# Expert rows of a mixture-of-experts layer in blocks of two 64-row halves instead of blocks of 128

## The chip, the core and the metric

The kernel runs on one core of one Trainium2 chip, as one program. The time is what the device takes for one execution, in microseconds (us). Five engines work side by side and meet at semaphores: TensorE (PE in the profile, with its weight loads as PEld), VectorE (DVE), ScalarE (ACT), GpSimd (POOL) and SyncE (SP, whose queue starts most transfers). Three runs of the kernel before gave 254.44, 252.72 and 254.32 us, median 254.32. All arithmetic is float32 but for a few small tables in bfloat16.

## What is computed

One decoder layer on 1024 tokens (8 tiles of 128) of width 256: latent attention, cross attention, and a feed-forward part, which is the part that changes. Cut to that part, the reference is:

```python
E, K, I, H = 16, 2, 176, 256                       # experts, chosen per token, hidden width, model width
x = hidden_states.reshape(-1, H)                   # 1024 tokens, layer-normed
scores = softmax(x @ gate_w.T)
topk_w, topk_idx = lax.top_k(scores, K)
combine = sum(one_hot(topk_idx, E) * topk_w[..., None], axis=1)
gu = einsum('th,ehj->etj', x, w_gate_up)           # 256 -> 352 per expert
h = silu(gu[..., :I]) * gu[..., I:]
y = einsum('eti,eih,te->th', h, w_down, combine)   # 176 -> 256 per expert
y = y + swiglu(x @ shared_gate_up) @ shared_down   # shared expert, for every token
```

Only the two experts of a token need be computed, so there are 2048 pairs of token and expert. For the inputs of the timed runs the sixteen experts get 69, 17, 81, 36, 112, 501, 135, 74, 592, 9, 104, 28, 62, 136, 18 and 74 of them (counted with the reference).

## The kernel before, in words

**Routing tables.** DVE, PE and POOL turn the router's choice into two lists of row numbers: for each row of a block the token to read (`idx[:, 0]`) and the place to write its result (`idx[:, 1]`). The pairs are sorted by expert, and every expert starts a new block of 128 rows, so 31 blocks are always enough (`BLOCKS`, L41). Here 25 hold rows; the last 6 are empty, but are computed all the same, since the program has no branch on the counts. The list of each block's expert (`bei`, L1549) is read by PE's sequencer into a register (`read_expert`, L917), and the register picks the weights in `gu_s` (up projection) and `dn_s` (down projection), which hold all sixteen experts.

**The expert loop.** A block of 128 rows passes through these steps: POOL gathers its rows from DRAM into one of four buffers (L487); PE transposes them with 2 products against the identity (`block_transpose`, L879) and DVE copies the result to `bxT` (`bT_out`, L1561); PE multiplies with the expert's up weights, 2 products over the two halves of the width (`expert_up`, L898); ACT takes the silu of one half (L1165), DVE multiplies it with the other (`h_mul`, L1567); PE transposes again (`hidden_transpose`, L889), ACT copies (`hT_out`, reported at L1000, the helper's line); PE multiplies with the down weights (`expert_down`, L910); ACT copies to `by` (`y_out`, L1000) and POOL scatters the rows to DRAM (L492). A float32 product appears as two records in the trace, a transpose as one. PE's order is written out (L974 to L987): in step i the hidden transpose of block i-2, the up projection of i, the row transpose of i+2, the down projection of i-3. Buffers alternate between two (PSUM banks, `bxT`, hidden) or four (`bx`, `by`).

**Around it.** The shared expert is worked in four pairs of token tiles with three column groups each (`shared_up`, L829, `shared_down`, L842). Two groups of the last pair stand behind the expert loop (L988, L989), and so do its 12 last products (L994). SP waits until every block with rows is back in DRAM (`written`, L385 to L387), then reads each token's two results (L389); DVE adds them with their weights (`weigh_pair`, L1574), adds the shared part (L1601), and SP and ACT write the output.

## Time and profile before

| | us |
|---|---|
| median of 3 runs | 254.32 |
| the profiled execution | 252.71 |
| its span, first to last instruction | 250.7 |
| PE busy in it, 1660 products | 237.4 |
| DVE busy | 148.5 |
| ACT busy | 129.3 |
| POOL busy | 92.5 |
| row gather of block 0 issued (L487) | at 157.61 |
| first up projection (L898) | at 164.43 |
| last output transfer issued (L1195) | at 248.32 |

Times in the rows further down count from the start of the span. A busy time of PE is the union of its records, and a record lasts beyond the moment at which the next product may start; the pace is therefore read from the starts. "idle before, releaser" in square brackets is how long the engine stood idle before a group and what ended it.

### The profile page before, as it was taken

To read this page: it belongs to the slowest core of one execution; us is meant where nothing else is said; L and a number is where in the kernel's file an instruction comes from. 1 tells how busy PE (TensorE), PEld (TensorE's weight loads), DVE (VectorE), ACT (ScalarE), POOL (GpSimd) and SP (SyncE) were. 2 spreads that over 40 slices of the span, in tenths; PEclk is the share of its full clock that TensorE was granted. 3 is DMA by queue.
4 is the path that set the end of the run, shared out by engine and by line. 5 is a ranking of instruction groups with operands and counts; after the bars stand their busy time and mean duration, and the time that the engine had idled before them with its cause. 6 is when DMAs were issued, how large, how long until landed. Compare 5 with 4: busy or idle time off the path is not lost.

```text
span 250.7 us, 5232 instructions
## 1 busy us (share of the span) xinstructions
PE 237.4 (95%) x1660; PEld 177.2 (71%) x1660; DVE 148.5 (59%) x452; ACT 129.3 (52%) x465; POOL 92.5 (37%) x110
## 2 busy tenths in 40 slices
PE   8969799999999999999999999799999999999995
PEld 6635475666766677898788787567777777777784
DVE  1568888887889856437896588653223232323184
ACT  2146988989889898540524216124343434343440
POOL 2111211112111100102662004655777777777460
PEclk9999999999999999999999999999999999999999
DMA  7999877100005400006013000222333333343495
GB/s 217 267 366 387 283 174 171 53 3 3 3 0 160 171 3 3 1 3 229 1 41 129 0 3 4 63 68 81 105 105 107 105 95 112 89 102 111 144 338 188
DMA packets 20388, 28.10 MB, mean 112 GB/s; under 512 B 2369, under 2 KB 17355, under 8 KB 20363
## 3 DMA queue, kind: packets, MB, share of 16 engines
q1 hardware_dynamic: 16683, 19.01, 24.5%
q0 software_dynamic: 2976, 8.13, 11.0%
q10 hardware_dynamic: 704, 0.64, 0.8%
q8 instruction: 14, 0.23, 0.4%
q14 instruction: 11, 0.09, 0.1%
HBM read 21.61 MB, written 6.16 MB: 111 GB/s over the span
## 4 chain that ended last, share of the span: by engine, by line
PE 71%; ACT 13%; DVE 8%; issue 4%; DMA 1%; POOL 1%; ACTq 0%; POOLq 0%; DVEq 0%
PE bank L898 15%; PE bank L910 11%; ACT pr_s L1010 10%; PE bank L829 8%; PE bank L531 5%; PE bank L573 4%; PE bank L560 3%; PE bank L879 3%; PE bank L889 3%; PE bank L658 2%; PE bank L536 2%; PE bank L623 2%; PE bank L649 1%; PE bank L668 1%; DMA qx_s<-ffn_in,prT 1%
## 5 line engine op out<-in xcount | busy, mean ns | idle before, releaser
L1010 ACT ACTIVATE pr_s<-bank,mx 128x128 f32<-128x128 f32 x128 | 45.2, 383 | 8.0 <-DVE mx L1236 8.0
L898 PE MATMUL bank<-gu_s,bxT 128*128 x124 | 41.7, 460 | 0.2 <-DVE bxT L1561 0.2
L1567 DVE TENSOR_TENSOR pr_s<-bank,pr_s 128x176 f32<-128x176 f32 x31 | 10.6, 341 | 51.6 <-ACT pr_s L1165 50.9
L492 POOL DMA_INDIRECT expert_out<-by,prT x31 | 31.0, 1000 | 14.8 <-ACT by L1000 7.5
L487 POOL DMA_INDIRECT qx_s<-ffn_in,prT x31 | 30.1, 972 | 14.6 <-issue 8.2
L1000 ACT ACTIVATE prT<-bank 128x512 f32<-128x512 f32 (+1 forms) x63 | 31.1, 497 | 2.9 <-PE bank L573 1.8
L910 PE MATMUL bank<-dn_s,prT 88*128 x124 | 31.7, 379 | 0.0
L1010 ACT ACTIVATION_READ_ACCUMULATOR pr_s<-bank,mx 128x1 f32 x128 | 28.6, 224 | 0.0
L898 PEld LDWEIGHTS bank<-gu_s,bxT 128*128 128x128 f32 x124 | 21.2, 190 | 7.2 <-issue 0.4
L1000 ACT ACTIVATE by<-bank 128x256 f32<-128x256 f32 x31 | 11.9, 383 | 23.5 <-PE bank L910 21.9
L1236 DVE TENSOR_REDUCE mx<-bank 128x4 f32<-128x512 f32 x32 | 20.5, 683 | 4.7 <-PE bank L560 4.7
L829 PE MATMUL bank<-ck_s,sgu_s 128*128 128x256 f32 (+1 forms) x96 | 22.0, 381 | 1.1 <-issue 1.1
L910 PEld LDWEIGHTS bank<-dn_s,prT 88*128 88x128 f32 x124 | 21.2, 190 | 2.2
L573 PE MATMUL bank<-tab,pr_s 128*128 128x128 f32 x128 | 19.5, 275 | 3.1 <-ACT pr_s L1010 2.7
L1165 ACT ACTIVATE pr_s<-bank 128x176 f32<-128x176 f32 x31 | 9.8, 317 | 24.3 <-PE bank L898 24.3
L573 PEld LDWEIGHTS bank<-tab,pr_s 128*128 128x128 f32 x128 | 15.0, 140 | 8.3 <-ACT pr_s L1010 4.0
L829 PEld LDWEIGHTS bank<-ck_s,sgu_s 128*128 128x128 f32 (+1 forms) x96 | 17.0, 181 | 4.6 <-issue 1.7
L414 POOL TENSOR_TENSOR rs<-ve,halfpow 128x2 f32<-128x2 f32 x8 | 5.6, 702 | 32.7 <-DVE ve L1276 32.7
L409 POOL TENSOR_TENSOR rs<-ve,halfpow 128x1 f32<-128x1 f32 x8 | 4.4, 554 | 33.3 <-DVE ve L1211 33.3
L1561 DVE COPY bxT<-bank 128x256 f32<-128x256 f32 x31 | 12.9, 415 | 3.7 <-PE bank L879 3.5
L1128 ACT ACTIVATE kbd<-bank 128x256 f32<-128x256 f32 (+1 forms) x12 | 4.6, 383 | 20.0 <-PE bank L829 20.0
L879 PEld LDWEIGHTS bank<-tab,qx_s 128*128 128x128 f32 x62 | 8.6, 140 | 8.1 <-issue 4.4
(194 smaller groups left out, 438.2 us busy)
## 6 DMA issues: line engine op xcount, KB each, us to landing
gu_s<-in_w_gu SPq DMA_DIRECT2D x8, 704.0 KB, 7.0
dn_s<-in_w_dn SPq DMA_DIRECT2D x4, 704.0 KB
gu_s<-in_ctx_in SPq DMA_DIRECT2D x2, 512.0 KB, 9.2
ffn_in<-x_s SPq DMA_DIRECT2D x4, 256.0 KB, 2.4
cv_s<-expert_out SPq DMA_DIRECT2D x4, 256.0 KB, 4.1
x_s<-expert_out SPq DMA_DIRECT2D x4, 256.0 KB, 5.7
out<-x_s SPq DMA_DIRECT2D x7, 128.0 KB, 3.6
gu_s<-in_x_t SPq DMA_DIRECT2D x1, 768.0 KB, 10.7
```

The lines of the kernel that those rows point to most:

```text
L487: pool.indirect_dma_start(bx[:, i % RB, :], None, ffn_in[:], bass.IndirectOffsetOnAxis(ap=idx[:, 0, i:i + 1], axis=0)).then_inc(dma_gather ...
L492: pool.indirect_dma_start(expert_out[:], bass.IndirectOffsetOnAxis(ap=idx[:, 1, k:k + 1], axis=0), by[:, k % RB, :], None).then_inc(dma_sc ...
L531: last = mm(bank[3][:, 0:NOPE + D], ckvT[:, b % 2, k, :], wkv_s[:, k, :], start=k == 0, stop=k == 1)
L573: last = tr(probs_bank(n)[:, h * T:(h + 1) * T], pr_s[:, n % 2, h, :], idf)
L829: last = mm(shared_bank(q, c)[0:r, 2 * j * T:2 * (j + 1) * T], sgu_s[:, k, j * SI + c * 128:j * SI + c * 128 + r], xfT[:, k, 2 * q:2 * q + ...
L879: last = tr(bank[6 + i % 2][:, k * T:(k + 1) * T], bx[:, slot, k * 128:(k + 1) * 128], idf)
L898: last = mm(bank[2 + i % 2][:, 0:2 * I], bxT[:, i % 2, k, :], gu_s[:, k, bass.ds(e, 1), :], start=k == 0, stop=k == KD - 1)
L910: last = mm(bank[4 + i % 2][:, 0:D], bhT[:, i % 2, k, :], dn_s[:, k, bass.ds(e, 1), :], start=k == 0, stop=k == 1)
L1000: copy = lambda o, i: nc.scalar.activation(o, i, ACT.Copy)
L1010: last = nc.scalar.activation(pr_s[:, n % 2, h, :], score_bank(n)[:, h * T:(h + 1) * T], ACT.Exp, bias=mx[:, n % 4, h:h + 1], accum_out=de ...
L1236: V.tensor_reduce(mx[:, n % 4, :], score_bank(n)[:].rearrange("p (h k) -> p h k", h=CH), op=ALU.max, axis=AX.X, negate=True).then_inc(dve_ ...
L1561: V.tensor_copy(bxT[:, i % 2, :, :].rearrange("p k t -> p (k t)"), bank[6 + i % 2][:, 0:D]).then_inc(dve_block_T, 1)
```

## The change

A block still has 128 rows, but they are two halves of 64, each with an expert of its own. The first 64 pairs of expert e lie in the upper half of block e, for e below 16, so that half's weights are known without a register. All further groups of 64 ("more" halves, at most 32) fill the lower halves of blocks 0 to 15, and both halves of blocks 16 to 23. There are 24 blocks (`BLOCKS`) and 48 halves (`HALVES`). With the counts above there are 26 "more" halves, so blocks 0 to 20 hold rows.

Each projection is now four products in place of two: 64 columns of weights-side data (`bxT[..., 0:HT]`, `bxT[..., HT:T]`) with output in partitions 0 to 63 or 64 to 127 of the same bank. The lower half takes its weights by register, the upper half by number. From block 16 on the upper half takes them from four staging buffers (`gu_x`, `dn_x`), which SP fills from DRAM with each expert's 352 KB and 176 KB; they lie over buffers of the first part of the layer (`early`). The weights lie in DRAM with the rows of a partition together.

PE, ACT and DVE go through the blocks in pairs. The second group of the last shared pair moves from behind the loop to its start, the third to between the up projection of block 23 and the last hidden transposes. The tables' arithmetic has a few more steps, and POOL's scatters trail its gathers by 10 blocks rather than 8.

```diff
+HT = T // 2
+MORE = 2 * ((SLOTS - 1) // HT // 2 + 1)
+BLOCKS = E + (MORE - E) // 2
+HALVES = 2 * BLOCKS
+SB = 4
+def more_of(i):
+    return i if i < E else E + 2 * (i - E)
...
+        staged = early[0][:, 0:SB * (KD * 2 * I + 2 * D)].rearrange("p (r n) -> p r n", r=SB)
+        gu_x = staged[:, :, 0:KD * 2 * I].rearrange("p r (k n) -> p r k n", k=KD)
+        dn_x = staged[0:IH, :, KD * 2 * I:].rearrange("p r (k n) -> p r k n", k=2)
...
+            sp.wait_ge(pe_expert_up, RB)
+            for j in range(BLOCKS - E):
+                e = staged_expert[j]
+                if j >= SB:
+                    sp.wait_ge(pe_expert_up, E + j - SB + 1)
+                sp.dma_start(gu_x[:, j % SB], w_gu[bass.ds(e, 1), :, :, :].rearrange("e p k n -> p (e k) n")).then_inc(dma_staged_up[j % SB], 16)
+                if j >= SB:
+                    sp.wait_ge(pe_expert_down, E + j - SB + 1)
+                sp.dma_start(dn_x[:, j % SB], w_dn[bass.ds(e, 1), :, :, :].rearrange("e p k n -> p (e k) n")).then_inc(dma_staged_down[j % SB], 16)
...
-            for k in range(2):
-                last = nc.gpsimd.tensor_tensor(num_b[:, 0, k * B:(k + 1) * B, :], num[:, k * B:(k + 1) * B, :],
-                                               tabr[:, R_TOK:R_TOK + B].unsqueeze(2).to_broadcast([128, B, BLOCKS]), ALU.mult)
-            last.then_inc(pool_block_numbers, 1)
-            LAG = RB + 4
+            nc.gpsimd.tensor_tensor(num_b[:, 0, 0:B, :], num[:, 0:B, :],
+                                    tabr[:, R_TOK:R_TOK + B].unsqueeze(2).to_broadcast([128, B, HALVES]), ALU.mult).then_inc(pool_block_numbers, 1)
+            LAG = RB + 6
...
                         for f in range(2):
-                            last = mm(bank[4][:, k * BLOCKS:(k + 1) * BLOCKS], hot[:, k * B + t, :],
-                                      num_b[:, f, k * B + t, :], start=t == 0 and f == 0, stop=t == B - 1 and f == 1)
+                            for u in range(2):
+                                last = mm(bank[4][u * HT:(u + 1) * HT, k * BLOCKS:(k + 1) * BLOCKS], hot[:, k * B + t, :],
+                                          num_b[:, f, k * B + t, u * BLOCKS:(u + 1) * BLOCKS],
+                                          start=t == 0 and f == 0, stop=t == B - 1 and f == 1, skip_group_check=True)
...
+                if i >= E:
+                    pe.wait_ge(dma_staged_up[(i - E) % SB], 16 * ((i - E) // SB + 1))
                 for k in range(KD):
-                    last = mm(bank[2 + i % 2][:, 0:2 * I], bxT[:, i % 2, k, :], gu_s[:, k, bass.ds(e, 1), :],
-                              start=k == 0, stop=k == KD - 1)
+                    mm(bank[2 + i % 2][0:HT, 0:2 * I], bxT[:, i % 2, k, 0:HT], gu_s[:, k, bass.ds(e, 1), :],
+                       start=k == 0, stop=k == KD - 1, skip_group_check=True)
+                    last = mm(bank[2 + i % 2][HT:T, 0:2 * I], bxT[:, i % 2, k, HT:T],
+                              gu_s[:, k, i, :] if i < E else gu_x[:, (i - E) % SB, k, :],
+                              start=k == 0, stop=k == KD - 1, skip_group_check=True)
...
+            pe.wait_ge(dve_block_experts, 1)
+            shared_up(PAIRS - 1, 0, between=range(RB - 1))
+            read_expert(RB - 1)
             block_transpose(0)
+            block_transpose(1)
...
             expert_up(1)
+            shared_up(PAIRS - 1, 1)
             block_transpose(2)
             block_transpose(3)
-            for i in range(2, BLOCKS):
+            for i in range(2, BLOCKS, 2):
                 hidden_transpose(i - 2)
+                hidden_transpose(i - 1)
+                if i + 2 < BLOCKS:
+                    block_transpose(i + 2)
+                    block_transpose(i + 3)
                 expert_up(i)
                 if i + 2 < BLOCKS:
-                    block_transpose(i + 2)
-                if i >= 3:
-                    expert_down(i - 3)
-                if i + 1 < BLOCKS:
-                    read_expert(i + 1)
+                    expert_up(i + 1)
+                expert_down(i - 2)
+                expert_down(i - 1)
+                if i + 2 < BLOCKS:
+                    read_expert(i + 2)
+                    read_expert(i + 3)
+                else:
+                    expert_up(i + 1)
+            shared_up(PAIRS - 1, 2)
             hidden_transpose(BLOCKS - 2)
...
-            link(V.tensor_scalar_mul(nb[:, 2, :], nb[:, 1, :], float(T)))
+            link(V.scalar_tensor_tensor(nb[:, 2, :], nb[:, 1, :], float(HT), tabr[:, R_BASE:R_BASE + E], ALU.mult, ALU.add))
...
+            link(V.scalar_tensor_tensor(t128[:, 0], rank, float(HT), nb[:, 2, :].unsqueeze(1).to_broadcast([128, B, E]),
+                                        ALU.is_ge, ALU.mult))
+            link(V.tensor_tensor(t128[:, 1], rank, t128[:, 0], ALU.add))
...
+            link(V.scalar_tensor_tensor(posf[:, 0, :], s8[:, 2:4, :].rearrange("p k t -> p (k t)"), float(HT), posf[:, 0, :],
+                                        ALU.mult, ALU.add))
```

**PE in the loop.** Before, one block of the loop on PE reads as follows (L889 hidden transposes, L898 up, L879 row transposes, L910 down, L918 the register's read; an ISA row sets an address from a register):

```order
L889 MATMUL bank<-tab,pr_s 88x128 x2
L898 ISA
L898 MATMUL bank<-gu_s,bxT 128x352
L898 ISA
L898 MATMUL bank<-gu_s,bxT 128x352
L879 MATMUL bank<-tab,qx_s 128x128 x2
L910 ISA
L910 MATMUL bank<-dn_s,prT 128x256
L910 ISA
L910 MATMUL bank<-dn_s,prT 128x256
L918 TENSOR_LOAD bei
```

Now a pair of blocks begins with eight transposes (L937, L927), and the up projections follow, lower half (L948) and upper half (L950) in turn:

```order
L937 MATMUL bank<-tab,pr_s 88x128 x4
L927 MATMUL bank<-tab,qx_s 128x128 x4
L948 ISA
L948 MATMUL bank<-gu_s,bxT 64x352
L950 MATMUL bank<-gu_s,bxT 64x352
L948 ISA
L948 MATMUL bank<-gu_s,bxT 64x352
L950 MATMUL bank<-gu_s,bxT 64x352
```

The second block's up projection and then both down projections follow in the same manner, and then two reads of registers: a pair has one row of transposes and one of projections, where it had four of each.

**SP ahead of the last reads.** SP's queue now has, from block 16's weights on, eight times this piece before it reads `ring_i` and waits for the rows with results:

```order
L426 ISA
L426 DMA early<-in_w_gu 128x704
L429 ISA
L429 DMA early<-in_w_dn 88x512
```

Before, these transfers weren't there: SP went from the writes of `ffn_in` to `ring_i` at once.

## Rows read from the trace of the kernel before

**Rows 1.** The page: chain of work that ended last, shares of the span by engine.
```profile
PE 71%; ACT 13%; DVE 8%; issue 4%; DMA 1%; POOL 1%; ACTq 0%; POOLq 0%; DVEq 0%
```
**Rows 2.** Windows of the trace: stretch, its length, busy time by engine, clock, DMA.
```profile
170.69:234.25 63.56, 63.56 (x309) 47.23 (x308) 17.48 (x52) 24.55 (x77) 46.30 (x48) 1.00 0.35 101
```
**Rows 3.** Timeline of one block: start us, us, engine, line, operation, tiles, count.
```profile
199.17 0.38 PE L889 MATMUL bank<-tab,pr_s 128*88 128x128 f32 x2
...
199.39 1.35 PE L898 MATMUL bank<-gu_s,bxT 128*128 x4
...
200.57 0.38 PE L879 MATMUL bank<-tab,qx_s 128*128 128x128 f32 x2
...
200.78 0.32 ACT L1165 ACTIVATE pr_s<-bank 128x176 f32<-128x176 f32 x1 [0.76 <-PE bank L898]
200.79 1.03 PE L910 MATMUL bank<-dn_s,prT 88*128 x4
...
201.12 0.34 DVE L1567 TENSOR_TENSOR pr_s<-bank,pr_s 128x176 f32<-128x176 f32 x1 [1.82 <-ACT pr_s L1165]
201.66 0.38 PE L889 MATMUL bank<-tab,pr_s 128*88 128x128 f32 x2
```
**Rows 4.** Timeline of PE round one group of 32-column products (L585).
```profile
66.48 0.60 PE L573 MATMUL bank<-tab,pr_s 128*128 128x128 f32 x4
67.01 1.08 PE L585 MATMUL bank<-prT,v_s 128*32 128x128 f32 x32
68.02 0.66 PE L542 MATMUL bank<-tab,qk 128*128 128x128 f32 x4
68.51 0.60 PE L573 MATMUL bank<-tab,pr_s 128*128 128x128 f32 x4
```
**Rows 5.** Timeline of PE: router products (32 columns) and shared-expert products (128).
```profile
139.14 1.07 PE L808 MATMUL bank<-ck_s,gate_s 128*32 128x256 f32 x16
...
148.82 5.34 PE L829 MATMUL bank<-ck_s,sgu_s 128*128 128x256 f32 x24
```
**Rows 6.** Timeline of POOL late in the expert loop.
```profile
225.35 0.97 POOL L487 DMA_INDIRECT qx_s<-ffn_in,prT  x1 [0.30 <-issue]
226.63 0.99 POOL L492 DMA_INDIRECT expert_out<-by,prT  x1 [0.30 <-issue]
```
**Rows 7.** Timeline of the routing tables and of the start of the expert loop.
```profile
148.43 0.28 DVE L1517 TENSOR_TENSOR qkT<-bank,nb 128x128 f32<-128x128 f32 x1
...
150.36 0.68 DVE L1525 TENSOR_TENSOR qx_s<-wm_s,posf 128x496 f32<-128x496 f32 x1
...
151.18 3.08 POOL L477 TENSOR_TENSOR qx_s<-qx_s,wm_s 128x248 bf16<-128x248 f32 x2 [15.94 <-DVE qx_s L1525]
...
154.36 0.96 PE L868 MATMUL bank<-qx_s 128*128 128x31 bf16 x32 [0.20 <-issue]
...
162.41 1.96 PE L829 MATMUL bank<-ck_s,sgu_s 128*128 128x256 f32 x8 [1.06 <-issue]
...
167.79 1.45 PE L898 MATMUL bank<-gu_s,bxT 128*128 x4 [0.17 <-DVE bxT L1561]
```
**Rows 8.** DMA issues: tiles, queue, count, KB each, median us from issue to landing.
```profile
gu_s<-in_w_gu SPq DMA_DIRECT2D x8, 704.0 KB, 7.0
...
wm_s<-in_w_m SPq DMA_DIRECT2D x1, 330.0 KB, 3.0
```
**Rows 9.** Timeline of the end: last useful rows out, their way back, last additions.
```profile
231.74 0.38 ACT L1000 ACTIVATE by<-bank 128x256 f32<-128x256 f32 x1 [0.77 <-PE bank L910]
...
234.83 1.94 SPq L389 DMA_DIRECT2D cv_s<-expert_out  x4
...
243.00 1.28 DVE L1574 SCALAR_TENSOR_TENSOR x_s<-x_s,s 128x256 f32<-128x256 f32 x3 [0.22 <-DMA x_s<-expert_out]
...
244.53 1.66 DVE L1574 SCALAR_TENSOR_TENSOR x_s<-x_s,s 128x256 f32<-128x256 f32 x4
...
247.43 0.86 DVE L1601 TENSOR_TENSOR x_s<-bank,x_s 128x256 f32<-128x256 f32 x2 [0.90 <-PE bank L994]
```

More of the change, by code:

```diff
@@ L13 @@
+import math
 import numpy as np
@@ L85, in routing_constants @@
     p = np.arange(128)[:, None]
-    c[:, R_THR:R_THR + B] = 128.0 * np.arange(B)
+    c[:, R_THR:R_THR + THRESHOLDS] = HT * (1.0 + np.arange(THRESHOLDS))
     c[:, R_LOW:R_LOW + E * E] = (np.arange(E)[None, :] < np.arange(E)[:, None]).reshape(1, -1)
-    c[:, R_BLK:R_BLK + BLOCKS] = np.arange(BLOCKS)
-    c[:, R_SLOT:R_SLOT + T] = np.arange(T)
+    lower = [E + more_of(i) for i in range(BLOCKS)]
+    upper = [i if i < E else E + more_of(i) + 1 for i in range(BLOCKS)]
+    c[:, R_BLK:R_BLK + HALVES] = lower + upper
+    c[:, R_SLOT:R_SLOT + HT] = np.arange(HT)
+    c[:, R_MORE:R_MORE + MORE] = np.arange(MORE)
+    c[:, R_BASE:R_BASE + E] = E * HT - HT - HT * np.arange(E)
     c[:, R_TOK:R_TOK + B] = T * np.arange(B)
     c[:, R_TOK + B:R_TOK + 2 * B] = p + 1
-    c[:, R_RING:R_RING + RB] = RB - 1 - np.arange(RB)
+    c[:, R_RING:R_RING + RB] = E + 1 + 2 * (RB - 1 - np.arange(RB))
+    c[:, R_RING + RB:R_RING + 2 * RB] = 2 * E + 2 * (RB - 1 - np.arange(RB))
     c[:, R_DUMMY:R_DUMMY + BLOCKS] = DUMMY + T * np.arange(BLOCKS) + p + 1
@@ L255, in decoder_layer @@
         dve_ring = sem("dve_ring")
+        dma_staged_up = [sem(f"dma_staged_up{i}") for i in range(SB)]
+        dma_staged_down = [sem(f"dma_staged_down{i}") for i in range(SB)]
         dve_first_sum, dve_second_sum, dma_out = sem("dve_first_sum"), sem("dve_second_sum"), sem("dma_out")
@@ L382, in _ @@
                              x1_s[:, 2 * q:2 * q + 2, :]).then_inc(dma_ffn_in, 16)
+            sp.wait_ge(dve_block_experts, 1)
+            staged_expert = [sp.value_load(bei[0:1, more_of(E + j) + 1:more_of(E + j) + 2], min_val=0, max_val=E - 1)
+                             for j in range(BLOCKS - E)]
+            sp.wait_ge(pe_expert_up, RB)
[7 more added lines that the diff above has]
+                sp.dma_start(dn_x[:, j % SB], w_dn[bass.ds(e, 1), :, :, :].rearrange("e p k n -> p (e k) n")).then_inc(dma_staged_down[j % SB], 16)
             sp.wait_ge(dve_ring, 1)
@@ L817, in logits_transpose, with shared_up @@
                 last.then_inc(pe_logits, 1)
-            def shared_up(q, c, halves=(0, 1)):
+            def shared_up(q, c, halves=(0, 1), between=()):
                 n, r = SC * q + c, shared_rows(c)
@@ L831, in shared_up @@
                                   xfT[:, k, 2 * q:2 * q + 2, :].rearrange("p b t -> p (b t)"), start=k == 0, stop=k == KD - 1)
+                        for i in between[KD * j + k:KD * j + k + 1]:
+                            read_expert(i)
                 if 1 in halves:
@@ L860, in slot_table @@
             def slot_table():
-                pe.wait_ge(dve_slot_hot, 1)
+                pe.wait_ge(dve_slot_hot, 2)
                 pe.wait_ge(pool_block_numbers, 1)
@@ L906, in expert_down @@
                     pe.wait_ge(act_expert_out, i - 1)
-                if i == 1:
-                    pe.wait_ge(dve_shared_hidden, SC * (PAIRS - 1) + 1)
+                if i < 2:
+                    pe.wait_ge(dve_shared_hidden, SC * (PAIRS - 1) + 2)
+                if i >= E:
+                    pe.wait_ge(dma_staged_down[(i - E) % SB], 16 * ((i - E) // SB + 1))
                 for k in range(2):
-                    last = mm(bank[4 + i % 2][:, 0:D], bhT[:, i % 2, k, :], dn_s[:, k, bass.ds(e, 1), :],
-                              start=k == 0, stop=k == 1)
+                    mm(bank[4 + i % 2][0:HT, 0:D], bhT[:, i % 2, k, 0:HT], dn_s[:, k, bass.ds(e, 1), :],
+                       start=k == 0, stop=k == 1, skip_group_check=True)
+                    last = mm(bank[4 + i % 2][HT:T, 0:D], bhT[:, i % 2, k, HT:T],
+                              dn_s[:, k, i, :] if i < E else dn_x[:, (i - E) % SB, k, :],
+                              start=k == 0, stop=k == 1, skip_group_check=True)
                 last.then_inc(pe_expert_down, 1)
@@ L1181, in _ @@
             silu(1)
-            for i in range(2, BLOCKS):
+            shared_silu(PAIRS - 1, 1)
+            for i in range(2, BLOCKS, 2):
                 hT_out(i - 2)
+                hT_out(i - 1)
                 silu(i)
-                if i >= 3:
-                    y_out(i - 3)
+                if i + 2 < BLOCKS:
+                    silu(i + 1)
+                y_out(i - 2)
+                y_out(i - 1)
+            silu(BLOCKS - 1)
+            shared_silu(PAIRS - 1, 2)
             hT_out(BLOCKS - 2)
-            y_out(BLOCKS - 3)
             hT_out(BLOCKS - 1)
@@ L1581, in _ @@
             h_mul(0)
+            h_mul(1)
             shared_add(2)
+            shared_mul(PAIRS - 1, 1)
             bT_out(2)
-            h_mul(1)
             bT_out(3)
             router_weights()
-            for i in range(2, BLOCKS):
+            for i in range(2, BLOCKS, 2):
+                if i + 2 < BLOCKS:
+                    bT_out(i + 2)
                 h_mul(i)
                 if i + 2 < BLOCKS:
-                    bT_out(i + 2)
+                    bT_out(i + 3)
+                h_mul(i + 1)
+            shared_mul(PAIRS - 1, 2)
             weigh_pair(0)
```

112 lines of the change are left out of this document (56 added, 56 removed).

## Prediction

> **What bounds the kernel now.** The chain that ended last is PE for 71% of the span [rows 1], so I looked for the stretch in which it is PE alone. In the expert loop the window of 63.56 us has PE busy for all 63.56 us, at the full clock of 1.00 (2.4 GHz), while DVE has 17.5 and ACT 24.6 us of work there; POOL, with 46.3 us, is the only other engine near it [rows 2]. Busy time of PE overlaps, so the pace has to come from starts. One block runs from the hidden transposes at 199.17 to the next at 201.66, 2.49 us, and that is 1.18 for the up projection (199.39 to 200.57), 0.87 for the down projection (200.79 to 201.66) and 0.22 for each of two pairs of transposes [rows 3]. These four fill the period, with nothing between them. ACT starts the silu at the end of the up projection (200.78) and DVE's product is done 0.7 us later (201.46), while the transposes that need it stand two steps on [rows 3]. So time in the loop falls only if PE streams less, and it then falls one for one until another engine is reached. At the end it is different: the way of the last useful rows back from DRAM lies beside PE's leftover products, and either may end last [rows 9].
>
> **Do two halves cost one block?** A record with 32 columns of stationary data starts a wave 0.11 us long, like one with 128 [rows 4]; narrow products save nothing by themselves. If the halves ran one after the other, a block's projections would take 4.1 us for 2.05. The loop of before has no 64-column product, so this comes from the nearest rows. The 32-column products of attention (16 products, 32 records, four column groups) go from 67.01 to the next line's start at 68.02 [rows 4]. At the 0.11 us of a 128-column record they would need 3.5 us one by one and 0.88 in eight waves of four: they overlap fully, both float32 passes included. The router's 16 records of 256 moving columns take 1.07 us with a tail of 0.38, so the waves start 0.23 apart, where 24 full products come every 0.216 ((5.34 - 0.38)/23) [rows 3, 5]. So the bounds for a half are 0 and 6% over a full product; I take 0, since in the longer run, rows 4, the waves keep the pace of full products.
> The Trainium skill, "TensorE: Matmul & The Clock Gate" (Part 3, measured speedup), speaks against that: it gives three column tiles a speedup of 2.38, not 3, or 79% per tile. By that an estimate for two tiles is 2.6 us for the 2.05, and most of the gain is gone. Rows 4 show no such loss, and I follow the rows.
>
> **Switching.** Entering the 32-column run costs 0.09 us (66.48 to 67.01, less four transposes of 0.11), its first wave and leaving it 0.13 (1.01 less 0.88), and the next transpose's start 0.05 (68.02 to 68.51, less 0.44): 0.28 us for in and out [rows 4]. The pairs need it once each. A pair is then 8 transposes 0.88 + 2 x 1.18 + 2 x 0.87 + 0.28 = 5.26 us, where two blocks took 4.98 [rows 3, 4]. Between 0.1 (part of it hidden) and 0.6 us per switch the pair is 5.1 to 5.6.
>
> **What hides beside it.** The chain up, silu, product, hidden transposes now has both down projections, 1.74 us, in front of its end, and needs 0.7 plus one 0.4 copy on DVE: slack of about 0.6. ACT has 2 x (0.32 + 0.38 + 0.38) = 2.2 of 5.26. POOL issues one transfer every 1.28 us [rows 6]; four per pair are 5.1 us, just under 5.26. It was 2.57 against 2.49 before, made up by its head start. The register reads stand between products that give them cover.
>
> **Start of the loop.** The tables: DVE has two operations grown from 128 to 240 elements (0.12 each, at 1.09 ns per element from 128 in 0.28 and 496 in 0.68), one more of 128 elements (0.31 with its gap), one of 16 (0.2), and the half numbers grow by 272 elements (0.30): +1.05. POOL's 3.08 us for 2 x 248 becomes some 2.4 for 384: -0.7. The slot products double in number; they take 0.96 if halves overlap, twice that if not, and I add 0.25. Together +0.6, between -0.3 and +1.6 [rows 7]. Up projection 2 started at 167.79. To that come 0.6, the moved shared group (8 records x 0.216 = 1.73) [rows 5] and its switch 0.3; PE's 1.06 us idle over three register reads goes [rows 7]; and a new wait comes in: DVE has the moved group's product in front of the copies of blocks 2 and 3, behind a silu on ACT. PE waits for these copies before row transposes 4 and 5 and up projection 2; I price it at 1.1 (silu 0.4, product 0.4, copy 0.4, less the hidden transposes), between 0 and 1.5. Sum: 170.4.
>
> **The loop itself.** Nine pairs lie between up projections 2 and 20: 170.4 + 9 x 5.26 = 217.8, where the old loop would have needed 18 x 2.49 = 44.8 for as many blocks, but went on to block 24 for the rows that now end in block 20.
>
> **The staged weights.** The first four go out ten blocks ahead. The sixth expert's up weights (for block 21) stand in SP's queue behind the down weights of the fifth, which wait for down projection 16. From that one's end to up projection 21 there are 0.87 + 0.88 + 0.28 + 1.18 = 3.2 us. A transfer of 330 KB on a nearly idle start took 3.0 us from issue, one of 704 KB in a full queue 7.0 [rows 8]; with half a microsecond for issuing the down weights (four issues in 1.94) [rows 9] the data come 3.5 to 7.5 us after that end, so PE stands still for 0.3 to 4.3. I take 1.2, since the queue is mostly empty there and the size is that of the 330 KB row. Blocks 22 and 23 have 4 us or more, and lie behind the useful rows.
>
> **The end.** Pair 22 begins at 217.8 + 1.18 + 1.2 + 1.18 + 1.74 + 0.1 = 223.2. Down projection 20 starts after 0.44 + 0.14 + 1.18, at 224.9; its copy out starts 1.07 later and takes 0.38, as at 231.74; and SP's reads start 2.71 us after that end (232.12 to 234.83): 229.1, or 5.7 earlier than before [rows 3, 9]. The last pair of token tiles then waits for its data. They came no earlier than 8.2 us after the reads began (243.00) and no later than 9.7 (244.53), when DVE was kept by the shared product anyway; I take 8.7, giving 237.8. Four weighings 1.66, two additions 0.86, and 2.4 from there to the end (248.29 to 250.7) give 242.7 [rows 9]. PE's own end: 11.3 us of work after 223.2, to 234.5, so it no longer sets the additions, which stood at 247.43 behind PE before. The span falls from 250.7 to 242.7, by 8.0: 5.7 in the loop, 2.3 behind it.
>
> **Rivals.**
> A, slower: **the halves do not overlap** when 352 columns stream through 64-column tiles. Each of 20 blocks costs 2.05 us more, +41, so about 287 us. Against it stand rows 4 and 5; for it, only that this shape is not in the trace. It decides from about 0.4 us per block on: 20 x 0.4 eats the 8 us. 4%.
> B: **they overlap in part**, a quarter slower than full products (0.37 for 0.29 us per record): +0.5 per block, +10, 255.5. That is the case of the skill's 2.38 for three. 5%.
> C: **POOL or DMA sets the pace.** POOL has 0.16 us of slack in a pair. If its issues take 1.2 instead of 0.98 us, the pair is 6.0 and nine of them add 7: 252.5. 6%.
> D: **staged weights come late** for block 21, at the 7.0 us of the large transfers: +3.1, 248.6. 9%.
> E: **the shared group's wait and the switches are hidden**, and the reads of the results, with three empty blocks' scatters beside them and not six, are faster: -3.5, 242. 10%.
> F: the change does nothing measurable, because the reads of results, not the loop, set the end. Against: they start when block 20 is written, and that moves. 2%.
> The forecast itself has 64%, with its own range of 242.5 to 249.5.
>
> **The numbers.** The profiled execution took 252.71 us, 1.6 under the median of 254.32. Less 8.0 this is 244.7 by the one and 246.3 by the other; the likeliest case is set between, at 245.5. Low end: E's 3.5 off gives 242, rounded to 241.5. High end: the forecast with switches at 0.5 (+2), the tables' upper bound (+1) and the late weights of D reach 251. That leaves out A, B, C and F. Some 1% (2.5 us) can be told from no change. Faster by over 1% are the forecast, D, E and half of C: 0.86. Within 1%: the other half of C, F and half of B, 0.07. Slower: A and half of B, 0.07.
>
> **What would show it.** In the profile after: up projections' records in twos a few ns apart and 0.29 us to the next two (else A or B); 5.2 to 5.3 us from pair to pair; up projection 2 near 170.4; an idle time of PE before block 21's up projection, released by a DMA; SP's reads near 229; the last additions released by DVE's own weighings, not by PE. Wrong would be a pair above 5.6, POOL without idle time in the loop, or reads that take over 10 us to land.

## The result, and the profile after

| | kernel before | changed kernel |
|---|---|---|
| median of the runs | 254.16 us (252.72 to 254.44, 4 runs) | 245.09 us (243.96 to 245.41, 4 runs) |
| profiled execution, its span | 252.71 us, 250.7 us | 245.34 us, 243.5 us |

The ratio is 0.9646, with a 95% interval of 0.9597 to 0.9695. The forecast was 245.5 us, between 241.5 and 251. In E2, in E6, in E10 and beside E11 (kernel before) one run each was slow and is left out of the medians and ranges given below. Of the span's 7.2 us, 5.45 are there when SP begins to read the results back (234.83 [rows 9], now 229.38), and 1.75 come behind that point.

The page of the changed kernel, chain of work that ended last, answers to [rows 1]:
```profile
PE 56%; ACT 14%; DVE 11%; DMA 8%; issue 5%; SPq 2%; POOL 2%; DVEq 0%; ACTq 0%; POOLq 0%
```
PE's share fell from 71% to 56% and DMA's rose from 1% to 8%: the chain now leaves PE for the staged weights of block 21 and for the last rows' way back. Up to there the loop is still PE alone. The window from up projection 2 to up projection 20, against [rows 2] (stretch, length, busy time by engine with records, clock, DMA share, GB/s):
```profile
170.30:217.50 47.20, 47.20 (x361) 27.39 (x360) 12.21 (x37) 17.87 (x54) 32.89 (x34) 1.00 0.53 151
```
PE is busy for all 47.20 us at the full clock (2.4 GHz). These are nine pairs of blocks, 5.25 us each. One pair in the timeline of PE (start us, us, engine, line, operation, tiles, count), against [rows 3]:
```profile
175.53 0.51 PE L948 MATMUL bank<-gu_s,bxT 128*64 x1
175.54 0.51 PE L950 MATMUL bank<-gu_s,bxT 128*64 128x352 f32 x1
175.88 0.46 PE L948 MATMUL bank<-gu_s,bxT 128*64 x1
175.89 0.46 PE L950 MATMUL bank<-gu_s,bxT 128*64 128x352 f32 x1
176.18 0.46 PE L948 MATMUL bank<-gu_s,bxT 128*64 x1
...
177.95 0.38 PE L965 MATMUL bank<-dn_s,prT 88*64 x1
177.96 0.38 PE L967 MATMUL bank<-dn_s,prT 88*64 88x256 f32 x1
...
179.78 0.64 PE L937 MATMUL bank<-tab,pr_s 128*88 128x128 f32 x4
180.26 0.60 PE L927 MATMUL bank<-tab,qx_s 128*128 128x128 f32 x4
180.79 0.51 PE L948 MATMUL bank<-gu_s,bxT 128*64 x1
```
L948 is the lower half, L950 the upper one. The upper record starts 6 to 7 ns behind the lower (the rows round to 10), and from the second two on the next two come after 0.29 to 0.30 us, the step of one full product of this width. So two halves with different weights take the time of one.

The start of the loop, timelines of DVE, POOL and PE, against [rows 7]:
```profile
151.16 0.96 DVE L1595 TENSOR_TENSOR qx_s<-wm_s,posf 128x768 f32<-128x768 f32 x1
...
152.26 1.68 POOL L522 TENSOR_TENSOR qx_s<-qx_s,wm_s 128x384 bf16<-128x384 f32 x1 [16.99 <-DVE qx_s L1595]
153.17 1.19 DVE L1600 TENSOR_TENSOR qx_s<-qx_s,wm_s 128x384 bf16<-128x384 f32 x1
...
154.41 1.19 PE L915 MATMUL bank<-qx_s 128*64 128x24 bf16 x64 [0.23 <-DVE qx_s L1600]
...
169.61 0.74 PE L927 MATMUL bank<-tab,qx_s 128*128 128x128 f32 x4 [0.48 <-DVE bxT L1635]
170.28 0.51 PE L948 MATMUL bank<-gu_s,bxT 128*64 x1
```
And the end, timelines of SP's queue, PE, ACT and DVE, against [rows 8, 9]:
```profile
216.43 0.34 SPq L426 DMA_DIRECT2D early<-in_w_gu  x1
...
220.34 0.51 PE L948 MATMUL bank<-gu_s,bxT 128*64 x1 [1.39 <-DMA early<-in_w_gu]
...
226.29 0.38 ACT L1063 ACTIVATE by<-bank 128x256 f32<-128x256 f32 x1 [0.55 <-PE bank L967]
...
229.38 1.96 SPq L435 DMA_DIRECT2D cv_s<-expert_out  x4
...
232.90 2.86 PE L1057 MATMUL bank<-sdn_s,v_s 128*128 128x256 f32 x12
...
239.31 1.27 DVE L1648 SCALAR_TENSOR_TENSOR x_s<-x_s,s 128x256 f32<-128x256 f32 x3 [0.45 <-DMA x_s<-expert_out]
240.50 0.75 DVE L1678 TENSOR_TENSOR x_s<-bank,x_s 128x256 f32<-128x256 f32 x2
```
The staged weights issued at 216.43 hold PE back once, for 1.39 us. The last additions (240.50) stand directly behind DVE's own weighings, and those behind data that landed (239.31); PE's last products began at 232.90. Before, the additions waited for PE [rows 9].

### The profile page after: what moved, and what is told of

Its sections match the earlier page's. It is cut to its first block, busy times and chain, and to the rows that moved or that the text cites. A ratio compares the mean times of both kernels' runs of the same rounds, so it can differ in the third digit from the quotient of the medians.

```text
span 243.5 us, 5429 instructions
## 1 busy us (share of the span) xinstructions
PE 223.9 (92%) x1800; PEld 156.7 (64%) x1800; DVE 144.6 (59%) x442; ACT 123.3 (51%) x444; POOL 77.1 (32%) x95
## 4 chain that ended last, share of the span: by engine, by line
PE 56%; ACT 14%; DVE 11%; DMA 8%; issue 5%; SPq 2%; POOL 2%; DVEq 0%; ACTq 0%; POOLq 0%
PE bank L948 11%; ACT pr_s L1073 10%; PE bank L965 7%; PE bank L873 5%; PE bank L575 5%; PE bank L617 4%; PE bank L604 3%; DMA x_s<-expert_out 3%; PE bank L702 3%; PE bank L937 2%; PE bank L927 2%; DMA bxT<-in_wh_t 2%; PE bank L580 2%; PE bank L667 2%; DMA early<-in_w_gu 1%
## 5 line engine op out<-in xcount | busy, mean ns | idle before, releaser
L948 PE MATMUL bank<-gu_s,bxT 128*64 x96 | 31.3, 466 | 1.4 <-DMA early<-in_w_gu 1.4
L536 POOL DMA_INDIRECT expert_out<-by,prT x24 | 23.7, 987 | 17.6 <-ACT by L1063 13.6
L1063 ACT ACTIVATE prT<-bank 128x512 f32<-128x512 f32 (+1 forms) x56 | 27.4, 514 | 2.7 <-PE bank L617 1.8
L531 POOL DMA_INDIRECT qx_s<-ffn_in,prT x24 | 23.4, 976 | 16.5 <-issue 8.9
L965 PE MATMUL bank<-dn_s,prT 88*64 x96 | 22.7, 379 | 0.4 <-ACT prT L1063 0.4
L948 PEld LDWEIGHTS bank<-gu_s,bxT 128*64 128x64 f32 x96 | 12.1, 136 | 14.5 <-issue 13.2
L950 PE MATMUL bank<-gu_s,bxT 128*64 128x352 f32 x64 | 20.6, 466 | 0.0
L965 PEld LDWEIGHTS bank<-dn_s,prT 88*64 88x64 f32 x96 | 13.0, 137 | 9.2 <-issue 3.7
L967 PE MATMUL bank<-dn_s,prT 88*64 88x256 f32 x64 | 15.1, 379 | 0.0
L575 PE MATMUL bank<-early 85*128 85x480 f32 x32 | 14.2, 566 | 0.0
```

The source lines that it names most:

```text
L531: pool.indirect_dma_start(bx[:, i % RB, :], None, ffn_in[:], bass.IndirectOffsetOnAxis(ap=idx[:, 0, i:i + 1], axis=0)).then_inc(dma_gather ...
L536: pool.indirect_dma_start(expert_out[:], bass.IndirectOffsetOnAxis(ap=idx[:, 1, k:k + 1], axis=0), by[:, k % RB, :], None).then_inc(dma_sc ...
L575: last = mm(bank[3][:, 0:NOPE + D], ckvT[:, b % 2, k, :], wkv_s[:, k, :], start=k == 0, stop=k == 1)
L948: mm(bank[2 + i % 2][0:HT, 0:2 * I], bxT[:, i % 2, k, 0:HT], gu_s[:, k, bass.ds(e, 1), :], start=k == 0, stop=k == KD - 1, skip_group_chec ...
L950: last = mm(bank[2 + i % 2][HT:T, 0:2 * I], bxT[:, i % 2, k, HT:T], gu_s[:, k, i, :] if i < E else gu_x[:, (i - E) % SB, k, :], start=k == ...
L965: mm(bank[4 + i % 2][0:HT, 0:D], bhT[:, i % 2, k, 0:HT], dn_s[:, k, bass.ds(e, 1), :], start=k == 0, stop=k == 1, skip_group_check=True)
```

## The experiments

They ran on four chips, and each is compared within its own chip. These differ: the kernel before took 252.74 us on the chip of E4 to E7, but 264.47 on that of E1 to E3, 262.64 on that of E8 to E10 and 264.10 on that of E11. What holds the changed kernel up on such a chip is the matter of E11; the kernel before was not traced on one.

**E1, order of the halves.** The same products, but all of the lower half ahead of the upper half's within a projection.
```
                 for k in range(KD):
                     mm(... lower half ...)
+                for k in range(KD):
                     last = mm(... upper half ...)
```


> The changed kernel, but within each projection both products of the lower half come first and then both of the upper half (before: lower and upper in turn). Open: how the two halves come to run side by side. Theory 1: products for the two column groups wait in separate lines, so program order within a projection does not matter; records of the two halves still start in twos, 0.29 us from two to two, a pair of blocks stays at 5.25 us and the time at 245 us, or at most 0.3 us per projection more where the ends of the two halves do not meet (20 blocks x 2 x 0.3 = +12 us at most). Theory 2: only neighbours in the program overlap; then each projection overlaps in one of its two products at best, a block's projections take 3.1 us or more for 2.05, and the time rises by 20 x 1.0 to 20 x 2.05, to 265 to 286 us.

253.74 us (one run; the kernel before 264.47 there). Timeline of PE:
```profile
176.37 0.51 PE L948 MATMUL bank<-gu_s,bxT 128*64 x1
176.38 0.51 PE L951 MATMUL bank<-gu_s,bxT 128*64 128x352 f32 x1
176.71 0.46 PE L948 MATMUL bank<-gu_s,bxT 128*64 x1
176.73 0.46 PE L951 MATMUL bank<-gu_s,bxT 128*64 128x352 f32 x1
```
Two windows of this run, an early pair and a later one:
```profile
175.40:180.70 5.30, 5.30 (x42) 3.49 (x42) 1.34 (x4) 1.68 (x6) 3.29 (x4) 1.00 0.93 264
191.40:197.50 6.10, 5.66 (x41) 3.60 (x42) 1.34 (x4) 1.72 (x6) 3.92 (x4) 1.00 0.27 86
```
Records still start in twos (13 ns apart here, 57 ns further on in the same pair), and an early pair takes 5.30 us for 5.25. The overlap does not need the halves to alternate in the program: the upper half's first record stands behind all four of the lower half in PE's order, and starts ahead of the second of them. The later pairs of 6.1 us, with PE idle, are not of this edit: the changed kernel has them too on such a chip (6.06 us in the run beside E8). The time of 253.74 us says little about the order itself: it is one run, the changed kernel was not run on this chip, and from 221.78 on, after a stop of PE of 1.89 us, the granted clock was 0.50 for 6.8 us.

**E2, full products.** Both halves use the lower half's expert in one product of 128 columns; the upper halves' own weights are left out of the computation.
```
-                    mm(bank[2 + i % 2][0:HT, ...], bxT[:, i % 2, k, 0:HT], gu_s[:, k, bass.ds(e, 1), :], ...)
-                    last = mm(bank[2 + i % 2][HT:T, ...], bxT[:, i % 2, k, HT:T], gu_s[:, k, i, :] ...)
+                    last = mm(bank[2 + i % 2][:, 0:2 * I], bxT[:, i % 2, k, :], gu_s[:, k, bass.ds(e, 1), :], ...)
```
(and the same for the down projection.)

> The changed kernel with its two 64-column products of each projection put back to one of 128 columns, both halves of a block using the lower half's expert (this leaves the upper halves' own weights out of the computation; the staged transfers still run and are waited for). It shows what splitting costs in all. Theory (halves overlap fully, only switching between 128- and 64-column products costs): a pair of blocks falls from 5.25 to 4.98 us, nine pairs and the start give -2.7 us, so 242.4 us. Rival (halves cost more than a full product, by contention or by more instructions): more than 0.5 us per pair falls away, -5 us or more.

249.72 us (248.63 to 250.98, 3 runs), ratio to the kernel before 0.944 (0.939 to 0.949). The 242.4 expected was for a chip like the first; the pairs are compared in its place. Windows of two pairs:
```profile
174.75:179.73 4.98, 4.98 (x27) 3.86 (x25) 1.34 (x4) 1.94 (x6) 3.13 (x4) 1.00 0.96 255
179.73:184.70 4.97, 4.97 (x26) 3.85 (x25) 1.34 (x4) 1.94 (x6) 3.23 (x4) 1.00 0.99 312
```
4.97 against 5.25: the halves cost 0.28 us a pair, all that the switches were priced at, and the products themselves cost nothing. One by one the halves of a pair would need 8.2 us (four times 1.18 + 0.87) for 4.1 [rows 3]; here they take 4.1 to 4.38 with the switch, a speedup of 1.87 to 2. The Trainium skill ("TensorE: Matmul & The Clock Gate", Part 3) gives 2.38 for three column tiles; for two tiles this trace shows no such loss.

**E3, one block at a time.** The order of before with the halves of now: each block's transposes and projections in turn.
```
-            for i in range(2, BLOCKS, 2):
+            for i in range(2, BLOCKS):
                 hidden_transpose(i - 2)
-                hidden_transpose(i - 1)
-                ... block_transpose(i + 3) ... expert_up(i + 1) ...
+                ... expert_up(i) ... block_transpose(i + 2) ... expert_down(i - 3) ...
```


> The changed kernel with the loop of before: block by block, hidden transposes of i-2, up projection of i, row transposes of i+2, down projection of i-3, on PE, ACT and DVE, with the 64-column halves kept. It shows what going two blocks at a time is worth. Theory (each way in and out of 64-column products costs PE 0.28 us): a block is 2.05 + 0.44 + 2 x 0.28 = 3.05 us, two are 6.1 for 5.25, so 20 blocks cost +8 us: 253 us, and nearly all of the change's gain is gone. Rival (switching is hidden behind the next weight loads or only costs once): two blocks stay under 5.5 us and the time within 2 us of 245.

258.26 us (256.93 to 259.08, 4 runs), ratio 0.977 (0.972 to 0.983), 8.5 us above E2. What the edit costs beside the changed kernel itself was not measured, since that was not run on this chip. Timeline of PE, two blocks:
```profile
173.03 0.51 PE L948 MATMUL bank<-gu_s,bxT 128*64 x1
...
174.37 0.44 PE L927 MATMUL bank<-tab,qx_s 128*128 128x128 f32 x2
174.74 0.43 PE L965 MATMUL bank<-dn_s,prT 88*64 x1
...
175.75 0.42 PE L937 MATMUL bank<-tab,pr_s 128*88 128x128 f32 x2
176.10 0.51 PE L948 MATMUL bank<-gu_s,bxT 128*64 x1
```
3.07 us a block, 6.13 for two, against 5.25. The loop now goes in and out of the 64-column products twice a block instead of once a pair, four times for two blocks: (6.13 - 4.97)/4 = 0.29 us each, by itself, the same as E2's 0.28. The grouping by two is worth 0.88 us a pair.

**E4, the changed kernel again,** with no edit, as the reference of its chip.

> The changed kernel itself, unchanged, as the reference for the kernels beside it on one chip. The first three experiments ran where the kernel before took 264.5 us and not 254.2, and there PE stood still in the loop behind ACT's copies out, which waited for the scatters of four blocks earlier. Theory: scatter landing differs from chip to chip, the pace of products doesn't; where the kernel before takes 254 us this one takes 245, with 5.25 us from pair to pair throughout; where it takes 264 us, this one shows pairs of over 6 us from the fourth on, with the copy to by waiting for a DMA. Rival: the difference to the first three lies in their edits alone; then this one keeps 5.25 us per pair everywhere.

245.79 us (245.25 to 248.72, 6 runs), ratio 0.974 (0.970 to 0.979). Pairs of 5.25 us and the same stop at block 21 (at 220.32). The time is close to that of the first measurement. The ratio is nearer to one because the kernel before is: nine of its eleven runs here have a mean granted clock of 1.00 and take 252.6 to 253.05 us, two have 0.992 and take 254.1 and 254.4; of its four runs in the first measurement, one took 252.72 and three 254.0 to 254.4.

**E5, five staging buffers.**
```
-SB = 4
+SB = 5
```


> The changed kernel with five staging buffers rather than four. The up weights for block 21 then no longer stand in SP's queue behind the down weights that wait for down projection 16. Theory (PE's idle 1.39 us before up projection 21 is that transfer's, and lies on the path to the end): it goes, and the time falls by 1.4 us beside the unchanged kernel on the same chip. Rival (the end is set by something that only happens to be later, the reads of results or POOL): the idle time goes and the time stays within 0.3 us.

243.56 us (243.16 to 245.86, 6 runs), ratio to before 0.964 (0.960 to 0.968); 2.2 below E4. No DMA wait stands at block 21, and SP's queue reads
```profile
221.09 0.32 SPq L429 DMA_DIRECT2D early<-in_w_dn  x1
227.68 1.96 SPq L435 DMA_DIRECT2D cv_s<-expert_out  x4
```
The reads start 1.9 us before those in E4's trace (229.57), and the span is 242.0 us for 243.4. The stop, 1.44 us there, was on the path in full.

**E6, the moved shared group behind the loop.**
```
-            shared_up(PAIRS - 1, 1)
             for i in range(2, BLOCKS, 2):
...
+            shared_up(PAIRS - 1, 1)
```
(with its silu and product, and another bank for its sums.)

> The changed kernel with the second group of the last shared pair put back behind the loop, next to the third (bank 7 as in the kernel before). Theory (PE has some 5 us to spare at the end, since the reads of results set it, while at the start of the loop the group costs 1.73 us, its switch 0.3 and the wait for DVE 1.1): the loop and all that follows come 3.1 us earlier, up projection 2 near 167.2, and the time falls by 3.1 us beside the unchanged kernel; PE's last products end by 235, still before the last weighings. Rival (the group only filled a time in which PE would have waited for the copies of blocks 2 and 3 or for gathered rows anyway): the loop starts under 1.5 us earlier and the time falls by less than 1.5.

243.46 us (243.05 to 245.78, 5 runs), ratio 0.965 (0.961 to 0.969); 2.3 below E4, not 3.1. The profiled execution took 247.61 us: it had a granted clock of 0.50 for 3.4 us from 18.91 on, ahead of what is read here, so only stretches are compared. Timeline of PE:
```profile
155.71 1.19 PE L915 MATMUL bank<-qx_s 128*64 128x24 bf16 x64 [0.23 <-DVE qx_s L1600]
...
168.91 0.39 PE L937 MATMUL bank<-tab,pr_s 128*88 128x128 f32 x2 [0.67 <-DVE x_s L1520]
...
170.04 0.51 PE L948 MATMUL bank<-gu_s,bxT 128*64 x1
```
From the slot products to up projection 2 it is 14.33 us for 15.87 in the changed kernel (15.77 in E4), 1.4 to 1.5 less and not 3.1. A part of what the group took comes back as a wait: with nothing in front of it, the second hidden transpose meets DVE's addition of a shared result (L1520), whose bank it needs. The other 0.8 us that the reads come earlier (72.86 us after the slot products for 75.12 in E4) arise behind up projection 2, where PE stands 0.79 us at block 21, for DVE, and not 1.44 for the weights.

**E7, the lag of the scatters,** back from ten blocks to the eight of the kernel before.
```
-            LAG = RB + 6
+            LAG = RB + 4
```


> The changed kernel with POOL's scatters 8 blocks behind its gathers, as in the kernel before, not 10: each scatter goes out some 2.7 us earlier. Theory (ACT's copy to by waits for the scatter of four blocks earlier where scatters land slowly, and each 0.1 us of that wait beyond the slack delays the hidden copies behind it and PE): on a chip where the kernel before takes 264 us the time falls by 3 to 8 us; on one where it takes 254 us by 0 to 0.5 us. Rival (the lag was raised because gathers would otherwise wait behind scatters for copies not yet made): PE waits for gathered rows and the time rises by 1 us or more.

248.62 us (246.46 to 249.76), ratio 0.980 (0.976 to 0.985); 2.8 above E4, as the rival had it. Timelines of POOL and of PE:
```profile
174.45 1.00 POOL L536 DMA_INDIRECT expert_out<-by,prT  x1 [2.26 <-ACT by L1063]
175.75 0.97 POOL L531 DMA_INDIRECT qx_s<-ffn_in,prT  x1 [0.30 <-PE bank L927]
...
182.80 0.44 PE L927 MATMUL bank<-tab,qx_s 128*128 128x128 f32 x2 [2.16 <-DMA qx_s<-ffn_in,prT]
```
A scatter waits for its rows, the gather stands behind it in POOL's queue, and lands 7 us later, beside the staged weights. PE stands 2.16 us, and that is not all: behind the stop the granted clock falls to 0.50 (1.2 GHz) for 3.4 us, and what PE does in them takes 1.7 us more. Window of the trace:
```profile
184.25:187.65 3.40, 3.40 (x16) 1.47 (x12) 1.11 (x4) 0.63 (x2) 0.30 (x1) 0.50 0.42 127
```
Up projection 6, at the stop, is 2.4 us later than in E4's trace (183.17 for 180.72), up projection 8 4.1 (190.11 for 185.98), and the reads 3.8 (233.41 for 229.57). The one number in this line is worth 2.8 us by the medians.

**E8 to E10, on one more chip.** E8 is E5 and E6 together; E9 is the changed kernel with the results read back in four transfers (four tiles of one expert) in place of eight (one tile of both), the bytes being the same; E10 is all three.
```
-            for t in range(B):
-                sp.dma_start(yg[t], ... "(k b p) d -> b p k d" ...[t])
+            for t in range(0, B, B // 2):
+                for k in range(2):
+                    sp.dma_start(four[:, :, k, :], ... [k][:, t:t + B // 2])
```
The changed kernel there:


> The changed kernel once more, as the reference of its chip for the three kernels run beside it. Both theories: 245 to 246 us if the scatters land as in its first run, pairs of 5.25 us, SP's reads near 229.4 us, the last additions near 240.5 us.

251.03 us (250.24 to 251.41, 5 runs), ratio 0.955 (0.952 to 0.958). It begins with pairs of 5.25 us, goes over to 6.06, and reads from 234.82 on, 5.4 later than in its first trace. My expectation of 245 to 246 had assumed a chip like the first.

E8:


> Five staging buffers and the second shared group behind the loop, together. Theory 1 (each takes away its own part of the path: the wait for block 21's weights 1.7 us, the moved group 1.5 us net of the wait that it uncovers): 3.2 us below the changed kernel of the same chip, the reads start at about 226.2 us and no DMA wait stands before up projection 21. Rival (PE's own leftovers now end last, since the group went from the loop's start to its end: the group's 1.7 us are only moved): the last products end near 234 to 236 us as before, so that the last additions are released by the product of the shared group and not by DVE's own weighings, and only 1.5 to 2 us are gained, no more than with the buffers alone.

248.92 us (248.13 to 250.20, 6 runs), ratio 0.948 (0.946 to 0.951): 2.1 below the changed kernel, the best of this chip. The last additions follow DVE's weighings, as theory 1 says; the 3.2 us don't come. Up projection 2 is 0.9 us earlier than in the changed kernel there (169.34 for 170.23), because the wait that E6 uncovers is 1.49 us and not 0.67:
```profile
168.34 0.39 PE L937 MATMUL bank<-tab,pr_s 128*88 128x128 f32 x2 [1.49 <-DVE x_s L1520]
```
The reads are 2.5 us earlier (232.35 for 234.82). The loop has waits of its own.

E9:


> The changed kernel with the reads of the results in four transfers (four tiles of one of the two experts each) in place of eight (one tile of both). The bytes are the same. Theory 1 (the last data are late because SP issues eight transfers in a row, some 0.5 us each, and the last one is issued 4 us after the first): the last two tiles' data arrive 1 to 2 us earlier, 244 us. Rival (the landing is set by the queues' work on 1024-byte and longer pieces, whatever the number of issues): the last data arrive at the same time, and the first tiles, which now wait for four tiles' data, start later: 0 to +1 us, 245.5 to 246.5.

253.28 us (251.80 to 253.95, 6 runs), ratio 0.964 (0.961 to 0.967), 2.25 above the changed kernel. DVE's timeline:
```profile
240.78 3.26 DVE L1650 SCALAR_TENSOR_TENSOR x_s<-cv_s,s,x_s 128x256 f32<-128x256 f32 x8 [2.43 <-DMA cv_s<-expert_out]
244.41 3.26 DVE L1650 SCALAR_TENSOR_TENSOR x_s<-x_s,s 128x256 f32<-128x256 f32 x8 [0.38 <-DMA x_s<-expert_out]
```
SP needs 2.05 us for its issues in place of 4.0, and the last data arrive 9.1 us after the first issue (235.34 to 244.41). In the changed kernel there the last read lands 9.7 after it (234.82 to 244.52). So issues that are 2 us shorter bring the last data 0.6 us forward, and small transfers let DVE start earlier: in the changed kernel it weighs from 237.79 on. From the first read to the last additions it is 12.25 us for 11.22; that 1.0 us is the edit's. The rest of the 2.25 is not: this trace has a granted clock of 0.50 for 3.4 us from 222.14 on, ahead of the reads, and the changed kernel's has none.

E10:


> All three edits together. Theory 1 (buffers, moved group and fewer issues each bring their own part): 1 to 2 us below the kernel with the first two. Rival (the landing is set by the queues, or the leftover products of PE end last by then): equal to the kernel with the first two, within 0.5 us, or up to 1 us above it.

249.75 us (249.42 to 251.18, 5 runs), ratio 0.953 (0.950 to 0.956), 0.8 above E8. The difference of the medians is hardly clear of the noise; in the traces it is the same as in E9, 12.05 us from the first read to the last additions for E8's 10.94.

**E11, eight result buffers.** From E1 and E8 I had read the pairs of 6.1 us as ACT's copies waiting for the scatter of four blocks earlier. Here E8 has eight buffers (YB = 8).
```
-                if i >= RB:
-                    act.wait_ge(dma_scattered[i % RB], 16 * (i // RB))
-                copy(by[:, i % RB, :], bank[4 + i % 2][:, 0:D])
+                if i >= YB:
+                    act.wait_ge(dma_scattered[i % YB], 16 * (i // YB))
+                copy(by_of(i), bank[4 + i % 2][:, 0:D])
```


> The kernel with five staging buffers and the moved shared group, and a ring of eight result buffers in place of four (by; four more slots in what the gathered rows' tile has free), everything else as it is. Theory 1 (the pairs of 6.1 us on the chips where the kernel before takes 262 to 265 us come from the copy to by waiting for the scatter of four blocks before; POOL's own issues need 5.1 us a pair): with eight buffers no copy waits, so pairs are 5.25 us whatever the chip; on such a chip 4.5 to 5.5 us below the kernel with four buffers (249 there), so a ratio to the kernel before of 0.925 to 0.935; on a chip where the kernel before takes 252 to 254 us nothing, some 242 us, ratio 0.955 to 0.96. Rival (the transfers themselves are slower there, gathers too, or POOL's queue holds both): the wait moves from the copy to the gathered rows or to POOL, pairs stay near 6 us, ratio 0.945 to 0.95.

251.21 us (249.32 to 251.84, 6 runs), ratio 0.951 (0.947 to 0.955): no gain over E8's 0.948. The traced execution has 3.4 us at a granted clock of 0.50 from 221.40 on, which E8's has not, so the pairs ahead of that decide. Windows of the trace:
```profile
174.40:184.90 10.50, 10.50 (x83) 6.08 (x82) 2.78 (x8) 2.98 (x11) 6.85 (x7) 1.00 0.97 291
190.30:196.50 6.20, 5.48 (x43) 3.00 (x41) 1.34 (x4) 1.72 (x6) 3.92 (x5) 1.00 0.26 85
```
The late pairs are as long as with four buffers (6.2 us for 6.07), so **my theory fell**. The rival's gathers and POOL don't explain it either: POOL has 3.92 us of work in 6.20, and PE waits for no gathered rows there. The timelines of PE, ACT and POOL show where the time is:
```profile
177.99 0.38 PE L970 MATMUL bank<-dn_s,prT 88*64 88x256 f32 x1
...
178.85 0.38 PE L970 MATMUL bank<-dn_s,prT 88*64 88x256 f32 x1
...
179.64 0.60 PE L930 MATMUL bank<-tab,qx_s 128*128 128x128 f32 x4
```
```profile
180.84 0.66 ACT L1066 ACTIVATE by<-bank 128x256 f32<-128x256 f32 x2 [2.65 <-remote]
...
181.30 0.97 POOL L534 DMA_INDIRECT qx_s<-ffn_in,prT  x1 [1.43 <-PE bank L930]
```
These are the results of blocks 2 and 3, whose copies wait for no scatter in this kernel. The last products began at 177.99 and 178.85, yet ACT stands idle until 180.84 and then does both copies at once. POOL's gather, which waits for the first block's row transposes, starts 1.66 us after these began (179.64). In the changed kernel's first trace the copies begin at 179.03 and 179.90, 0.43 us after their last products' starts, and the gather at 180.91, 0.65 after its transposes' start. So on this chip ACT and POOL learn 1.0 to 2.4 us late that PE is done.

As far as the trace tells, the lateness lies on PE's side. It keeps the time of each update of a semaphore, and in the changed kernel's first trace the update for a down projection stands 0.40 us after its last product's start, for all 24 blocks. Here it is 0.51 and 0.40 us for blocks 0 and 1, but 2.83 and 2.06 for blocks 2 and 3 (180.82 and 180.91), and the one for the row transposes goes from 0.29 to about 3 us in the pairs behind. In E8 the same updates are late by as much from block 2 on, and at 0.40 again in the last blocks. ACT's copy starts 0.02 us and POOL's gather 0.26 us behind its update, as in the first trace.

What delays PE's updates stays open. PE reads two registers from SBUF in every pair, and the late updates follow these reads; but a copy at 228.25, 1.3 us after the last of them, is on time:
```profile
228.25 0.38 ACT L1066 ACTIVATE by<-bank 128x256 f32<-128x256 f32 x1 [0.55 <-PE bank L970]
```
No run takes the reads away; that wasn't tried, and E11 ran on one chip only.

## Why the prediction was right

**Halves as one block**: right, and the decisive step. Forecast for the pair 5.26, measured 5.25; rivals A and B are out by the records in twos and by E2. **The switch**: 0.28 forecast, 0.28 (E2) and 0.29 (E3) measured. **Nothing else reaches PE in the loop** on this chip: PE is busy for 47.20 of 47.20 us, where I had left POOL 0.16 us of slack. C is out: POOL's issues wait for PE and ACT (32.89 us of work in that window), not the reverse.

**Start of the loop**: 170.4 forecast, 170.28 measured, from terms that were each off; that they meet is luck. The tables cost +0.62 at the first gather (158.23 for 157.61, 0.6 forecast), but the slot products began only 0.05 later (154.41 for 154.36, where the sum had 0.35; POOL's operation took 1.68 us and not 2.4), and from there to the gather it took 0.57 more, for 0.25 in the sum. The price of the moved group was too high: 1.73 + 0.3 + 1.1 us in the sum, 1.4 to 1.5 by E6. By E6 up projection 2 would stand at 168.8 without the group; the sum has 167.3, so the rest was as much too low. The group fills time in which PE would wait for DVE anyway; "what does PE wait for once this is gone" was not asked.

**Staged weights**: 1.2 us forecast, 1.39 measured at block 21, and by E5 1.4 of the span (medians: 2.2). The landing was nearer to the 3.0 of the 330 KB row, 3.6 us from issue in the chain, than to the 7.0 of D.

**The end**: reads at 229.1 forecast, 229.38 measured, 2.71 us after the copy's end as before. The mis-sized term is their landing: I took 8.7 us to the last wait for data, from a range of 8.2 to 9.7, and it was 9.9 (239.31), outside the range. The trace before had the answer: its last read landed at 244.35, 9.5 after the first issue. Less than all of this shows in the span (243.5 for 242.7), because three weighings were left behind the last wait and not four: +0.3 for the reads' start, +1.2 for the landing, -0.5 for the weighings, -0.2 from there to the end. E9 shows that fewer issues are no way to get it back. Rival E had these reads faster; in this it is wrong in its sign.

**The number.** The sum gave 244.7 by the profiled execution and 246.3 by the median, and 245.5 was set between. The span fell by 7.2 us and not by 8.0, and the time by 7.4 from one profiled execution to the other (252.71 to 245.34), but by 9.1 from median to median: three of the four runs before took 254.0 to 254.4, times that on E4's chip go with a mean clock of 0.992. So the closeness of 245.5 to 245.09 is in part luck. The high end, added up again, is 251.6 (245.5 + 2 + 1 + 3.1), not 251.

**What no step priced**: the raised lag, which the prediction passed over, and without which 2.8 us are lost (E7: a stop of 2.16 us and 1.7 of lower clock behind it); and the chip. The forecast holds for a chip like that of the runs shown ahead of it. Where the kernel before takes 262 to 265 us, PE waits in the loop and the changed kernel takes 251.03, just outside the range; the gain is larger there, 4.5% for 3.5% (and 2.6% on the chip of E4).

## What to carry over

If two groups of rows each fill half of the columns of a product and PE is the bound, put them side by side: float32 products of 64 columns with different weights cost one wide product, plus 0.28 us for each way in and out of the narrow ones, so collect the narrow ones in runs. Price a moved piece of work by what its engine would wait for without it, not by its length alone. Count a stop of PE with the clock behind it: in E7 2.16 us of waiting brought 1.7 more. And before reading a wait as that of the buffer that the code names, give it more buffers: here one run refuted that reading.

## What the runs showed of the hardware

Two float32 products of 64 columns overlap even when the program issues all of one half first (E1: starts 13 to 57 ns apart). The kernel before takes 252.6 us on one chip and 261.97 on another, at a mean granted clock of 1.00 in both runs; on the slower chips the changed kernel's PE updates its semaphores late in most of the loop (0.40 us after a down projection's last product on the first chip, 2.06 to 3.81 for blocks 2 to 11 of E11). The granted clock fell to 0.50 for 3.4 to 6.8 us behind stops of PE of 1.78 to 2.16 us in E1, E2, E7, E9 and E11, but not behind stops of 1.75 to 1.82 in E8, E10 and the changed kernel beside them, nor behind one of 2.33 in E2. And eight reads in 4.0 us of issues have their last data 9.7 us after the first issue, four reads of twice the size in 2.05 us 9.1 after.
